# Nine extra matmuls on TensorE around the energy sum of a spectral attention block

## The reference, cut to what matters

```
xa_n = inorm(xa)                                   # every image by its own mean and variance
k, q = spec_conv(xa_n, kw), spec_conv(xa_n, qw)    # 8+8 x 8 low modes, kept at 64 x 64
v    = spec_conv(xa_n, vw)                         # the same modes, kept at 256 x 256
att  = softmax(q k^T * 64) v                       # over the 64 images of the batch
att  = inorm(att) + xa
att_n = inorm(att)
mix  = spec_conv(att_n, mix_w) + skip * att_n      # 32+32 x 32 modes
out  = inorm(inorm(mix)) + att
x    = x + out
```

## Time and profile before

| | us |
|---|---|
| median of 3 runs | 634.36 (633.36 to 634.97) |
| the profiled execution, whole | 633.88 |
| its span, first to last instruction | 632.1 |
| TensorE busy | 581.8 (92%) |
| VectorE busy | 482.8 (76%) |
| ScalarE busy | 356.6 (56%) |
| GpSimd busy | 336.4 (53%) |
| mean DMA rate | 226 GB/s, 142.55 MB |

### The profile page before, as it was taken

One profiled execution on the slowest core, in us unless ns is written; L12 is line 12 of the kernel. 1 busy time (PEld: TensorE's weight loads), 2 busy tenths in 40 slices (PEclk: granted clock), 3 DMA queues, 4 the chain that ended last, 5 costly groups with the idle time before them and its releaser, 6 DMA issues.

```text
span 632.1 us, 13832 instructions
## 1 busy us (share of the span) xinstructions
PE 581.8 (92%) x5072; PEld 480.6 (76%) x5072; DVE 482.8 (76%) x1095; ACT 356.6 (56%) x778; POOL 336.4 (53%) x398
## 2 busy tenths in 40 slices
PE   9999996999999996999999999699999999866994
PEld 9999644899899842789999874488999985354773
DVE  4666787787776888688777768777877768878996
ACT  6888353575666534466666635256576662543431
POOL 0270046959960014896975002597897200479993
PEclk9999996999999999899999999789999999979998
DMA  8993003899899901579999950279799993005787
GB/s 318 326 385 110 1 2 96 293 311 301 292 313 322 328 14 41 208 264 305 287 332 309 317 206 1 67 255 303 252 334 322 322 303 112 0 34 192 263 309 270
DMA packets 75522, 142.55 MB, mean 226 GB/s; under 512 B 6016, under 2 KB 6656, under 8 KB 75456
## 3 DMA queue, kind: packets, MB, share of 16 engines
q1 hardware_dynamic: 75456, 141.67, 65.6%
HBM read 74.54 MB, written 67.11 MB: 224 GB/s over the span
## 4 chain that ended last, share of the span: by engine, by line
PE 53%; DVE 25%; ACT 7%; POOL 5%; DMA 5%; issue 5%; SPq 0%; DVEq 0%; ACTq 0%; POOLq 0%
PE psY L386 23%; PE psP L448 15%; PE psT L433 7%; DVE QP L945 6%; DVE X L909 4%; ACT SQ L604 3%; POOL X L855 3%; DMA X<-in_x 3%; DVE Y L909 3%; DVE SQ L909 3%; DMA out<-X 2%; PE psP L494 1%; DVE IM L913 1%; DVE SQ L919 1%; DVE IM L916 1%
## 5 line engine op out<-in xcount | busy, mean ns | idle before, releaser
L855 POOL TENSOR_TENSOR X<-X,ALPHA 128x512 f32<-128x512 f32 x244 | 254.6, 1080 | 31.7 <-DVE IM L1142 18.5
L386 PE MATMUL psY<-FWD,X 128*128 128x128 f32 x1856 | 224.0, 279 | 2.3 <-DMA X<-in_x 2.2
L386 PEld LDWEIGHTS psY<-FWD,X 128*128 128x128 f32 x1856 | 213.1, 193 | 15.5 <-issue 13.9
L945 DVE TENSOR_REDUCE QP<-SQ 128x32 f32<-128x512 f32 x256 | 162.2, 680 | 48.3 <-ACT SQ L604 48.1
L909 DVE TENSOR_TENSOR X<-X,psP 128x512 f32<-128x512 f32 x192 | 125.8, 684 | 51.2 <-PE psP L448 23.9
L448 PE MATMUL psP<-INVW,T 64*128 64x256 f32 x768 | 141.9, 404 | 13.4 <-DVE X L909 7.8
L604 ACT ACTIVATE SQ<-X 128x512 f32<-128x512 f32 x232 | 132.4, 621 | 9.1 <-DVE Y L916 6.4
L833 POOL TENSOR_TENSOR Y<-Y,OMEGA 128x256 f32<-128x256 f32 x32 | 24.5, 765 | 189.0 <-ACT Y L612 189.0
L448 PEld LDWEIGHTS psP<-INVW,T 64*128 64x128 f32 x768 | 93.8, 191 | 34.2 <-ACT T L630 14.8
L630 ACT ACTIVATE T<-psT,BIA,SCL 128x256 f32<-128x256 f32 x128 | 65.3, 560 | 94.3 <-PE psT L433 89.8
L596 ACT ACTIVATE Y<-psY 128x512 f32<-128x512 f32 x128 | 76.2, 595 | 46.5 <-PE psY L386 45.3
(11 more groups left out here) (206 smaller groups left out, 552.5 us busy)
## 6 DMA issues: line engine op xcount, KB each, us to landing
X<-in_x SPq DMA_DIRECT2D x116, 512.0 KB, 5.4
out<-X SPq DMA_DIRECT2D x116, 512.0 KB, 3.9
X<-in_x SPq DMA_DIRECT2D x24, 256.0 KB, 4.2
Y<-in_x SPq DMA_DIRECT2D x6, 1024.0 KB, 5.1
out<-X SPq DMA_DIRECT2D x24, 256.0 KB, 3.8
INVH<-t_inv_h SPq DMA_DIRECT2D x1, 256.0 KB, 8.8
LW<-in_low_w SPq DMA_DIRECT2D x1, 204.0 KB, 5.7
FWD<-t_fwd SPq DMA_DIRECT2D x1, 128.0 KB, 2.1
```

What stands on the lines that cost most here:

```text
L386: last = mm(psY[p % 2][:, (2 * i + c) * 128:(2 * i + c + 1) * 128], image(nb, 2 * p + i)[:, a, c * 128:(c + 1) * 128], FWD[:, a, :], start ...
L855: P.tensor_tensor(v, v, al, MUL).then_inc(x_scaled, 1)
L945: V.tensor_reduce(QP[:, 4 * (k % 2) + place(n) % 4, :], SQ[:, n % RING, :].rearrange("p (a g j) -> p g a j", a=HC, j=GW), AX.XY, ADD).then ...
```

## The change

`warm` is called at two more places in `attend`: four matmuls after the last mode products and ahead of `energy(b, 0)`, and five between `energy(b, 0)` and `spread(b, 0)`. That is 9 per batch and 36 in all, each 128 x 128 against 256 columns. No wait, no semaphore and no other instruction is changed.

```diff
-WARM = (2, 4)
+WARM = (2, 4, 4, 5)
...
                 raw_modes(b, 3, (1, 2, 3))
+                warm(WARM[2])
                 energy(b, 0)
+                warm(WARM[3])
                 spread(b, 0)
                 turn_low(b, 0)
                 turn_modes(b, 3)
```

## The result

The changed kernel takes 631.39 us (median of 10 runs, 629.80 to 632.09) against 633.86 us for the kernel before in the same comparison (10 runs, 632.52 to 635.17). The ratio is 0.9957, with a 95% interval from 0.9942 to 0.9972: 2.5 us, or 0.4%, faster. Forecast were 632.4 us and a gain of 2.0 us; about half a us of the distance to 632.4 is the kernel before, which was taken at 634.36 us and came out at 633.86 here.

A forecast was written before the change was run, and what follows sets the result against it. GpSimd's images, then the late loads, were taken to bound the kernel behind 41 us of half clock. Four spread gains of 0.5 us and zero for TensorE's lead gave 631.9, plus 0.48 for the median: 632.4 us, range 629.8 to 635.0.

The forecast's parts named there:

- The extra matmuls cost nothing: Around the energy sum: 5.2 us of TensorE idle time hides the nine matmuls, ending 0.5 and 0.3 us early.
- The clock: Behind the energy sums: idle time shrinks to 0.5 + 0.3 us, so the four half-clock stretches, 41 us, are gone.
- the wait of 3.45 us: Batch 3, ahead of 581.50: TensorE's idle stretch read as passing at full clock, supporting the clock step.
- The spread, 0.5 us per batch: Spread's two matmuls ahead of C2 run at full clock, shifting GpSimd's whole list; 4 x 0.5 = 2.0 us.
- I give it zero: TensorE's lead behind the spread brings nothing by the batch's end; upper bound 1.1 us in batches 0 and 2.
- The sum: Whole kernel: 633.88 - 2.0 = 631.9 us for the profiled execution, forecast median 632.4 us.
- the lead is kept: Rival at the end of batches 0 and 2: 1.1 us more gained in each, 630.2 us; chance 0.15.
- The energy sums stay 151.94 us apart: Sign of a wrong prediction: distance between successive batches' energy sums unchanged, where 151.4 us was forecast.
- closer than 151 us: Sign of a wrong prediction: successive batches' energy sums closer than this, where 151.4 us was forecast.
- The fifth stretch: Last batch, half clock from 582.6 to 586.0 after a 3.45 us wait; should stay, at its place or moved.
- Each us of it is worth about half a us: Last batch: price given to any change in length of the fifth half-clock stretch.
- The rule of the Trainium skill: Prices lost clock as throttled time multiplied by one half, some 20 us here; the prediction did not follow it.

The follow-up runs named there:

- eight: Changed kernel with eight unread matmuls instead of five between energy sum and spread; ratio 0.9998 against the kernel before.
- five alone: Changed kernel with the five matmuls behind the energy sum but without the four ahead of it; ratio 0.9995 against the kernel before.
- the run with the spread late: Changed kernel with one more unread matmul between the wait for the coefficients and the spread's first matmul in each batch; ratio 0.9977 against the kernel before.
- half stores: Kernel before and changed kernel, both with the second half of every stored row left out; 626.96 us and 624.91 us.
- `warm(4)` at inverse_h: Changed kernel with four more unread matmuls ahead of each batch's first inverse_h; ratio 0.9958 against the kernel before.
- a delay put in behind the first quads: Changed kernel with six unread matmuls ahead of the forward of pair 4 in the first three batches; 636.92 us, ratio 1.0059 against the kernel before.
- with two matmuls: Changed kernel with two unread matmuls ahead of the forward of pair 4 in the first three batches; 633.44 us, ratio 0.9974 against the kernel before.
- its repetition: The kernel before run once more without edit, with a second profile; ratio 0.9997.
- the kernel with thirteen matmuls in the last batch: Changed kernel with thirteen more unread matmuls in batch 3, three of them ahead of its second energy sum; 628.11 us, ratio 0.9899 against the kernel before.

## Why the prediction was right, and where it was not

The extra matmuls cost nothing. Right: they ended 0.52 and 0.41 us before they were in the way (0.5 and 0.3 forecast), and the runs with eight and with five alone show what holds that up. The cover is thin, and the five need the four ahead of the energy sum. The four without the five were not run.

The clock. Right: in the two profiles of the changed kernel no stretch at half clock is left in the 14 us behind any of the four energy sums. The one exception among the variants with all nine is the run with the spread late, with 3.4 us from 5.9 us after the last energy sum on. One ground for it was weak: the wait of 3.45 us in the earlier trace rows was read as passing at full clock, but half clock began 1.1 us after it.

The spread, 0.5 us per batch. Right: 0.45, seen in the first factors, in the first reload of batches 0 and 1, and, with late loads out of the way, as 150.31 against 149.86 with half stores. The run with eight shows that a shift of the spread reaches the end of the kernel.

"I give it zero", the lead behind the spread. This is the step that failed. The comparison of batches 0 and 1, 151.94 us each, looked like two equal results of unequal work; the further profiles show that one batch scatters by 0.7 us, so two equal distances could not carry a zero. The lead has two parts. What TensorE gains up to the end of the first quad is worth nothing, because GpSimd's images come after it (`warm(4)` at inverse_h: ratio 0.9958). What a long stretch costs beyond that, 0.9 to 1.1 us at the late mark, is not worth nothing: with the spread later than before the kernel was still faster (0.9977), and a delay put in behind the first quads was paid, 6.9 us of 7.7. The likely reason, argued from the kernel's order and not shown by itself, is that each load of the last pairs waits for a store that waits for TensorE's own images, so that with two matmuls the waits for loads moved along instead of covering the delay. How much of the 1.1 us comes through is open: the distances of the kernel before don't show it, and its executions as a whole point to about 1.0 us for 6.8 us more of half clock.

The sum. With 0.45 a batch and the whole 1.1 for each long stretch it is 1.8 + 2.2 = 4.0 us for the profiled execution of before, which had two, and 1.8 + 1.1 = 2.9 for its repetition, which had one. Measured were 2.5 us in the first comparison and 0.0042 to 0.0068 as a ratio over three, 2.7 to 4.3 us. The two profiled executions themselves lie 2.1 us apart, with 1.75 of it in the tail. The forecast lay inside its range and its gain of 2.0 was somewhat short, on the side of the rival "the lead is kept", which had 630.2 us. It came so close partly by luck: the term that was put at nothing is small against the rest in most executions. An estimate says how small: the granted clock is 0.965 in the mean of 91 executions of before and 0.9925 in 24 of the changed kernel and the one with `warm(4)`, which is some 35 us less at half clock, where four short stretches make 27 and each long one 6.8 more. If the rest of the span lost the same in both, about one stretch in four was long, and the sum is near 1.8 + 1.1 = 2.9 us. The share of either part in the measured 2.5 us stays open.

The signs. "The energy sums stay 151.94 us apart" was named as showing the prediction wrong, and in the first profile they did (151.83, 152.35, 152.25); in the second one of them came closer than 151 us (150.43), the other such sign. With this scatter neither could decide anything from one profile. The mean over five profiles, 151.53 against 152.33, is as near to the forecast 151.4 as it can tell.

The fifth stretch stayed, as forecast, at its place or moved. "Each us of it is worth about half a us" was right only where it covers the last work ahead of the second spread: 3.4 us at 582.6 went with 1.85 us more on the way to the last finish, 3.4 us at 577.8 with nothing.

The rule of the Trainium skill ("TensorE: Matmul & The Clock Gate", section "HAM oscillation — how this bites in real kernels"), half of the throttled time, would have given some 20 us for the four places. The measured gain disagrees. The whole clock brought back in all five places, in the kernel with thirteen matmuls in the last batch, gave 6.7 us by medians (628.11 against 634.81 for the kernel before in that comparison).

## What to carry to other kernels

Lost clock is priced by what ends last behind it: here 41 us at half clock held 0.45 us a batch on the path and, when a stretch was long, up to 1.1 more. The matmuls that only hold the clock had to cover the idle time on both sides of a small piece of work here, and to end before the data came: they had 0.4 us of slack, and 0.8 us too much took the whole gain. And two batches of one profile that agree are not yet a proof: where one batch scatters by 0.7 us, as here with the DMAs at a 0.93 share, compare over several profiles.

## What the runs showed that was not expected

The same program gave stretches of 6.8 and of 13.7 us at half clock after the same idle time, in different batches in each profile, although TensorE was busy for 10.58 of the 13.7 us. The same 3.4 us of half clock in the last batch went with 1.85 us more or with none, depending on which matmuls they covered.
